# Layer d's 31-tap filter moved from VectorE to GpSimd, in six pieces

## What is computed

```
v      = silu(dwconv(hs @ v_proj_w.T, v_conv_w))        # [b, l, 4 heads, 64]
delta  = delta_rule(q, k, v, beta)                       # needs inverses of triangular 16x16 blocks
fir    = lambda x, w: dwconv(x, w)                       # causal, one filter per channel
short  = fir(v, fir_short_w)                             # 3 taps
long_  = fir(v, fir_long_w)                              # 31 taps
gate_in = concat([hs, short.mean(2), long_.mean(2), delta.mean(2)])
wgt    = softmax(gelu(gate_in @ fg_w1.T + fg_b1) @ fg_w2.T + fg_b2)   # then a floor, and normalised
o      = wgt0 * short + wgt1 * long_ + wgt2 * delta + wgt3 * v
```

## Time and profile before

| | |
|---|---|
| median of 3 runs | 4395.78 us (4394.23 to 4397.10) |
| profiled execution | 4401.85 us, its span 4399.9 us |
| PE, DVE, ACT, POOL busy | 77%, 60%, 37%, 7% of the span |
| granted TensorE clock, mean | 0.887 of full |
| taps of both filters on DVE | 1024 instructions of line 1790 and 64 of line 1788, 473.1 us |

### The profile page before, as it was taken

One profiled execution on the slowest core, in us unless ns is written; L12 is line 12 of the kernel. 1 busy time (PEld: TensorE's weight loads), 2 busy tenths in 40 slices (PEclk: granted clock), 3 DMA queues, 4 the chain that ended last, 5 costly groups with the idle time before them and its releaser, 6 DMA issues.

```text
span 4399.9 us, 64768 instructions
## 1 busy us (share of the span) xinstructions
PE 3407.8 (77%) x22532; PEld 2643.9 (60%) x22532; DVE 2618.4 (60%) x5927; ACT 1639.0 (37%) x3066; POOL 315.0 (7%) x696
## 2 busy tenths in 40 slices
PE   1687878787887878788787888878788887878854
PEld 0465757566675756567575666657566665756652
DVE  4336484756748475674847557484665738466553
ACT  1333333443333434333334433333433333444311
POOL 1001010100101010010101001010100101010010
PEclk7788989899999989999898899999889899989966
DMA  2020111101111110101111011111001111100100
GB/s 84 1 68 25 63 33 63 32 23 45 30 63 33 63 32 25 44 28 63 32 63 32 16 48 33 63 32 63 18 22 57 33 63 32 51 22 29 52 13 3
DMA packets 183454, 175.67 MB, mean 40 GB/s; under 512 B 58952, under 2 KB 147680, under 8 KB 183136
## 3 DMA queue, kind: packets, MB, share of 16 engines
q1 hardware_dynamic: 183136, 171.27, 12.2%
HBM read 156.55 MB, written 14.68 MB: 39 GB/s over the span
## 4 chain that ended last, share of the span: by engine, by line
PE 49%; DVE 25%; issue 11%; ACT 7%; POOL 5%; DMA 2%; SPq 1%; DVEq 0%; PEldq 0%; PEld 0%; ACTq 0%; POOLq 0%
PE bank L699 27%; DVE region L1790 8%; PE bank L733 6%; PE bank L787 3%; DVE region L1749 2%; ACT pt_f L1194 2%; PE bank L754 2%; PE bank L767 2%; POOL region L679 2%; POOL region L677 2%; DVE nm_f L1571 2%; ACT split_f L1205 1%; PE bank L708 1%; PE bank L1013 1%; DMA gram_scratch<-region 1%
## 5 line engine op out<-in xcount | busy, mean ns | idle before, releaser
L1194 ACT ACTIVATE pt_f<-bank 128x512 f32<-128x512 f32 x768 | 416.0, 595 | 274.8 <-PE bank L767 274.1
L699 PE MATMUL bank<-xTb,c_w 128*128 128x256 f32 x2048 | 498.3, 401 | 0.0
L699 PE MATMUL bank<-c_w,region 128*128 128x256 f32 x2048 | 465.6, 381 | 0.0
L1790 DVE SCALAR_TENSOR_TENSOR region<-vpad,cols,region 128x256 f32<-128x256 f32 x1024 | 451.9, 483 | 16.0
L699 PEld LDWEIGHTS bank<-xTb,c_w 128*128 128x128 f32 x2048 | 408.7, 203 | 69.7 <-issue 10.4
L1723 DVE SCALAR_TENSOR_TENSOR yb<-bank,comb,yb 128x256 f32<-128x256 f32 x256 | 112.1, 479 | 531.3 <-PE bank L699 531.3
L1293 ACT ACTIVATE region<-bank,cols 128x256 f32<-128x256 f32 x512 | 212.8, 470 | 568.2 <-PE bank L699 568.2
L699 PEld LDWEIGHTS bank<-c_w,region 128*128 128x128 f32 x2048 | 384.8, 190 | 51.7 <-issue 0.2
L733 PE MATMUL bank<-identb,split_f 128*102 128x128 bf16 (+1 forms) x4096 | 315.8, 248 | 101.6 <-DVE split_f L1556 81.0
L733 PEld LDWEIGHTS bank<-identb,split_f 128*102 128x102 bf16 (+1 forms) x4096 | 300.2, 149 | 131.6 <-issue 85.4
L767 PE MATMUL bank<-qT_f,kT_f 102*128 102x256 bf16 (+1 forms) x1536 | 281.7, 284 | 121.3 <-ACT pt_f L1194 97.0
(11 more groups left out here) (305 smaller groups left out, 5744.8 us busy)
## 6 DMA issues: line engine op xcount, KB each, us to landing
c_w<-in_c_w SPq DMA_DIRECT2D x256, 512.0 KB, 4.6
gram_scratch<-region SPq DMA_DIRECT2D x16, 512.0 KB, 2.6
x<-in_x SPq DMA_DIRECT2D x16, 256.0 KB, 4.4
ctxf<-in_ctx SPq DMA_DIRECT2D x16, 256.0 KB, 4.6
ctxb<-in_ctx SPq DMA_DIRECT2D x16, 256.0 KB, 6.8
out_dram<-x SPq DMA_DIRECT2D x16, 256.0 KB, 2.2
region<-gram_scratch SPq DMA_DIRECT2D x128, 8.0 KB
inverse_scratch<-region SPq DMA_DIRECT2D x32, 64.0 KB
```

Source lines behind the costliest of these rows:

```text
L699: mm = pe.matmul(out_ap, l, r, start=(i == 0), stop=(i == len(pairs) - 1))
L1194: act.activation(dst, PS[use].rearrange("p (c s) -> p c s", c=c), func, **kw).then_inc(*PS.drained(use))
L1790: ins = dve.scalar_tensor_tensor(dst[:, c, :], x, w_[:, c, k:k + 1], dst[:, c, :], ALU.mult, ALU.add)
```

## The change

GpSimd gets the 31 taps. The first is one multiplication of 128 x 512 by the weights; each later one is two `tensor_scalar` of 128 x 256 into a new buffer `fir_tmp` and one `tensor_tensor` of 128 x 512 that adds it. A `link` stands behind the pair and another behind the sum. The list `POOL_TAPS` cuts the taps into pieces of 5, 9, 5, 4, 4 and 4, which stand in POOL's stream at `d_token`, `d_chan`, `d_fir0`, `d_fir1`, `d_fir2` and `d_fir3`. VectorE keeps the 3 short taps, now at `d_fir2`, `d_fir4` and `d_fir6`, and waits for POOL's last tap in `d_sums`.

```diff
--- before.py
+++ after.py
@@ -45,6 +45,7 @@
 EPS = 1e-5
 NEG = -4.0e9
 LEVELS = 7
+POOL_TAPS = (0, 5, 14, 19, 23, 27, 31)
 BASE = 4
 BB = 1 << BASE
 NBK = P // BB
@@ -377,6 +378,7 @@
         blkX, blkT, blkU = (low[:, i * 256:(i + 1) * 256].rearrange("p (r c) -> p r c", r=BB) for i in range(3))
         blkT2 = low[:, 256:768]
         blk_tmp = low[:, 768:832]
+        fir_tmp = sb("fir_tmp", [P, C, S])
         sums = region[:, 2048:2048 + 3 * S].rearrange("p (a s) -> p a s", a=3)
         fshort, flong, qn, kn, kb, vb, vt, uu, dd = (sub(2, S) for _ in range(9))
         beta = sb("beta", [P, T, DH])
@@ -434,6 +436,7 @@
         d_T0 = signal("d_inverse_begun", NBK, 16)
         d_fir = signal("d_fir_ready", 1)
         d_sum2 = signal("d_filter_sums", 1)
+        d_firp = signal("d_fir_gpsimd", 1)
         d_half = signal("d_half_turned", 1)
         d_z = signal("d_logits", 1)
         d_ez = signal("d_gate_exp", 1)
@@ -663,10 +666,28 @@
             def layer_d(b):
                 done[0] = 0
                 pool.sem_clear(s_blocks)
+                def taps(lo, hi):
+
+                    w_ = col("firl").rearrange("p (c k) -> p c k", c=C)
+                    for k in range(lo, hi):
+                        if k == 0:
+                            link(pool.tensor_tensor(flong[:, :, :], vpad[:, :, 0:S], w_[:, :, 0:1].to_broadcast([P, C, S]), ALU.mult))
+                        else:
+                            for c in range(C):
+                                ins = pool.tensor_scalar(fir_tmp[:, c, :], vpad[:, c, k:k + S], w_[:, c, k:k + 1], None, ALU.mult)
+                            link(ins)
+                            ins = pool.tensor_tensor(flong[:, :, :], flong[:, :, :], fir_tmp[:, :, :], ALU.add)
+                            link(ins) if k < POOL_TAPS[-1] - 1 else ins.then_inc(*d_firp.up)
+
+                yield "d_token"
+                pool.wait_ge(*d_silu(b))
+                taps(POOL_TAPS[0], POOL_TAPS[1])
                 yield "d_norm"
                 pool.wait_ge(*d_ss(b))
                 pool.tensor_tensor(rn[:, :, :, :], ss[:, :, :, :],
                                    neghalf[:, 0:16].rearrange("p (a t h) -> p a t h", a=2, t=T), ALU.pow).then_inc(*d_rn.up)
+                yield "d_chan"
+                taps(POOL_TAPS[1], POOL_TAPS[2])
                 yield "d_blocks"
                 step = lambda ins: link(ins)
                 step(pool.tensor_copy(blkT, eye[:, :, :]))
@@ -678,6 +699,14 @@
                                             blkT[:, j, 0:m_].unsqueeze(1).to_broadcast([P // 2, n_, m_]), ALU.mult))
                     step(pool.tensor_tensor(blkT[:, j + 1:, 0:m_], blkT[:, j + 1:, 0:m_], tmp, ALU.subtract))
                 pool.tensor_copy(blkU, blkT.rearrange("p r c -> p c r")).then_inc(*d_blocks_inv.up)
+                yield "d_fir0"
+                taps(POOL_TAPS[2], POOL_TAPS[3])
+                yield "d_fir1"
+                taps(POOL_TAPS[3], POOL_TAPS[4])
+                yield "d_fir2"
+                taps(POOL_TAPS[4], POOL_TAPS[5])
+                yield "d_fir3"
+                taps(POOL_TAPS[5], POOL_TAPS[6])
                 yield "d_out"
                 pool.wait_ge(*d_ms(b))
                 pool.tensor_tensor(rn[:, 0, :, :], ss[:, 0, :, :],
@@ -1790,7 +1819,7 @@
                             ins = dve.scalar_tensor_tensor(dst[:, c, :], x, w_[:, c, k:k + 1], dst[:, c, :], ALU.mult, ALU.add)
                     return ins
 
-                taps = [(fshort, ws, KS, k) for k in range(KS)] + [(flong, wl, KL, k) for k in range(KL)]
+                taps = [(fshort, ws, KS, k) for k in range(KS)]
                 def filters(i, n):
 
                     for k in range(i * len(taps) // n, (i + 1) * len(taps) // n):
@@ -1828,6 +1857,7 @@
 
                 yield "d_sums"
                 dve.wait_ge(*d_fir(b))
+                dve.wait_ge(*d_firp(b))
                 for par in range(2):
                     dve.wait_ge(*PS.filled(f"d_Q{LEVELS - 1}{par}", b))
                 for i, x in enumerate((fshort, flong)):
```

## The result

The changed kernel takes 5204.6 us, the kernel before 4395.0 us on the same chip: 1.1845 times as long (95% interval 1.1824 to 1.1866). The forecast of 4670 us had the sign and the place right, and a third of the size. It is 810 us more, 51 us for each of the 16 bodies with part d.

The account below looks back on a forecast made before the run. POOL's chain to `f_res`, then DVE's filter, were taken to bound the kernel. POOL's overrun of 19 us less 2 saved gave 17 us per body, 272 us over 16 bodies: 4396 + 272, rounded to 4670 us, range 4450 to 4880.

Parts of the forecast that it names:

- What bounds the kernel now: Part d: POOL's chain through the inversion to `f_res`'s root, up to 1629, then DVE's filter up to `a_out`.
- The price of a tap: Each later tap on POOL: two `tensor_scalar` of 0.45 us, a sum of 1.15, links 0.16; 2.2 us, between 1.55 and 2.9.
- The engines' waiting for each other: POOL waits for DVE's two-input instructions: 5 us up to `f_res`, 1 us behind it, the whole between 0 and 10.
- the sum: Per body with part d: 19 us late less 2 us saved, 17 us; over 16 bodies 272 us.
- Step 5: POOL's last twelve taps, 26.4 us: `a_res`'s root starts at 1675.6 instead of 1655.1, `a_apply` on DVE 19 us late.
- The 12 us that `d_one4` was to wait: PE at `d_one4`, 1642.85 before, waits some 12 us for scattered blocks arriving at about 1658.
- What is given back: Behind `a_apply`, DVE without the filter of `d_fir5` saves 2 us before `rest_f`; nothing counted for `d_fir6`.
- The signs: Changed profile: POOL busy some 1300 us, DVE some 450 less, about 20 us idle before each apply, body 274 us.
- POOL's taps are dearer: Rival for POOL's stream: 2.6 us a tap and 10 us of waiting, 33 us a body, 4925 us; chance 0.17.
- The path over SP and `d_one4`: SP stores blocks only after f's output, 19 us later, delaying PE; wants `a_res`'s root at some 1666 to 1670.

Follow-up runs that it names:

- twelve taps: Against the kernel before, GpSimd does only 12 taps, as tensor_tensor pairs, ahead of the block inversion; VectorE does the other 19: 4527.8 us, ratio 1.0283.

## Why the prediction was wrong, point by point

- *What bounds the kernel now.* Right. POOL's chain through the inversion to `f_res`, and on to `a_res`, is where the time went; the two early pieces and the late ones each delay it as traced.
- *The price of a tap.* This is the step that failed: "I take 0.45 us, between 0.30 and 0.60" for `tensor_scalar`. It is 0.92 undisturbed. A tap is 3.27 us and not 2.2, outside even the upper end of 2.9, and 30 x 1.07 = 32 us per body. The addition was right to 0.11 us (1.26 undisturbed, 1.15 taken). The bound was drawn from instructions that have the same number of inputs but do no arithmetic, and I let them speak for one that does. What an instruction of POOL costs went with its form: copy, broadcast product and `tensor_scalar` of 512 elements take 0.61, 1.04 and 1.56 us.
- *The engines' waiting for each other.* I had 6 us on POOL. In the body shown, the pairs of line 677 that took longer than 1.82 us, the sums above 1.26 and the root of `d_norm` above 2.90 exceed these times by some 4.9 us in all. This was right for the changed kernel. What the sharing costs VectorE has no term in the sum, nor in any rival's, although the prediction names it. VectorE's instructions are the same in the changed kernel and in the one with a single long tap, and they are busy for 2319.3 and 2201.7 us: 118 us, over 7 per body, which lie behind POOL's longer stream. Without that cover (twelve taps) the chain through VectorE is 10 us longer, more than the 8 us per body that are lost.
- *Step 5.* The root of `a_res` came 50.7 us late instead of 20.5; the tap explains 32, the smaller waiting takes back 1.1. The 12 us that `d_one4` was to wait do not follow from the prediction's own times (1658 less 1642.85 is 15); it waits 26.5.
- *"What is given back."* Wrong: 2 us was counted, none came. From `a_apply` to `rest_f` it took 6.7 us before and takes 6.6 now, because TensorE's transposes and products between them run at the lower clock behind the wait (1.11 and 3.78 us instead of 0.60 and 1.99). Another 2.2 us are lost right behind, from `rest_f` to the split (3.0 us before, 5.25 now): TensorE's doubling products ran beside `d_fir5` before, and are now waited for. The first group of them still runs at a granted clock of 0.50, 1.92 us instead of 1.05.
- *The signs.* POOL was to be busy for some 1300 us and was for 1866; a body was to last 274 us and lasts 307. VectorE's busy time was to fall by some 450 us and fell by 299; in the kernel with a single long tap it fell by 417. Its idle time before `f_apply` and `a_apply` was to be about 20 us each and is 31.8 and 14.6.
- The sum with these terms: 17 + 32 - 1.1 + 1.9 + 2.2 = 52 us per body, measured 51.
- *The rivals.* "POOL's taps are dearer" had the right mechanism, but its 4925 us again rest on too cheap a tap, 2.6 us. The path over SP and `d_one4` was real: in the kernel with the early pieces alone it sets the time.

## What to carry to other kernels

Before work is moved to an engine that seems idle, the length of each instruction form has to be measured on that engine in the shape that it will have; a copy or a fill of the same size is no substitute. An engine that does short steps for others is not idle between them: what a piece put ahead of such a step overruns its gap by is paid for, here in full, and a piece that fits into the gap can still hold up the other engine through shared reads. And what a filter of 452 us busy time is worth is told by a kernel without it: here 0.7%, which another cut of the same list on the same engine gained as well.

## What the runs showed of the hardware that I had not expected

- GpSimd's `tensor_scalar` in fp32 takes 2.5 ns per element and some 0.28 us to start, with a number per partition (468 ns for 64 elements, 922 for 256, 1562 for 512). With a constant it takes 848 ns for 256. The product with a broadcast column is a third cheaper: 612 ns for 256, 1041 for 512.
- VectorE's two-input instructions of 704 elements take up to twice as long beside GpSimd's taps (0.89 and 1.83 us; the means of the three lines hit are 1.31 to 1.48) and stay at 0.89 beside its fills. One-input instructions are not spared: the two `tensor_scalar` of 704 elements take 1.12 and 1.09 us on average beside taps, 0.53 before, and one of 16 elements takes 0.92 to 1.23 us in all 16 bodies, where it took 0.17 in the body shown before.
